# Decoder layer on one core: all engines' work lists reordered, PSUM banks reassigned, max and score groups of opposite rows placed side by side

## What is computed

```python
def attn(x):                      # 16 heads of 16
    q = (layernorm(x, qn) @ Wq + bq) * scale ; k, v = layernorm(x, kvn) @ Wkv + bkv
    q, k = rotary(q, norm(x)), rotary(k, norm(x))      # rotated, then layernorm per head
    w = softmax(where(causal, layernorm(q) @ layernorm(k).T / 4, min))
    return (w @ v) @ Wo + bo
def xattn(x, enc):                # the 64 positions are features, the 256 features positions
    q, k, v = split(x.T @ w_in.T + b_in)               # 8 heads of 8, 256 x 256 scores
    o = softmax(where(band, q @ k.T / sqrt(8), min)) @ v
    return (relu((o @ w_out.T + b_out).T) * enc) @ w_ct + b_ct
def ffn(x):                       # weights quantised to three levels in groups of 64
    gate, up = split(x @ ternary(w_gate_up).T)
    return rms_norm(silu(gate) * up) @ ternary(w_proj).T
x = layernorm(x + attn(x)); x = layernorm(x + xattn(x, ctx)); x = layernorm(x + ffn(x))
```

## Time and profile before

| | before |
|---|---|
| median of three runs | 899.84 us (898.8 to 900.99) |
| the profiled execution | 899.05 us |
| its span on the core | 897.3 us |
| busy PE / POOL / DVE / ACT | 819.0 / 760.4 / 762.2 / 653.7 us |
| mean granted clock of TensorE | 0.974 |

### The profile page before, as it was taken

How to read it: one execution, slowest core, us unless ns; L and a number is a source line. 1 busy time by engine, 2 the same in 40 slices (tenths; PEclk the granted TensorE clock), 3 DMA queues, 4 the chain that set the end, 5 groups by cost and what they waited for, 6 DMA issues and landing times.

```text
span 897.3 us, 23809 instructions
## 1 busy us (share of the span) xinstructions
PE 819.0 (91%) x9618; PEld 493.9 (55%) x9618; DVE 762.2 (85%) x1495; ACT 653.7 (73%) x1171; POOL 760.4 (85%) x879
## 2 busy tenths in 40 slices
PE   3779998899999999999999999999999999889885
PEld 1334555455566655665666665666666665545442
DVE  4699988888989999998998999999999998767663
ACT  1356567667878888888887887888888888756763
POOL 5498889978999999999999999999999987544741
PEclk9889999999999999999999999999999999988998
DMA  7000111111233333322222222233333332223333
GB/s 249 12 7 14 45 46 30 39 32 35 66 67 73 73 73 73 72 67 67 69 65 59 66 65 66 68 66 72 73 73 73 67 68 67 61 60 67 54 85 86
DMA packets 125029, 57.64 MB, mean 64 GB/s; under 512 B 93044, under 2 KB 124020, under 8 KB 124920
## 3 DMA queue, kind: packets, MB, share of 16 engines
q1 hardware_dynamic: 124920, 56.12, 27.5%
HBM read 13.62 MB, written 4.19 MB: 20 GB/s over the span
## 4 chain that ended last, share of the span: by engine, by line
PE 48%; DVE 15%; POOL 15%; SPq 11%; DMA 6%; ACT 3%; issue 2%; POOLq 0%; DVEq 0%
PE ps L741 6%; SPq L299 5%; PE ps L710 4%; POOL hsum L2142 4%; PE ps L669 3%; PE ps L561 3%; DMA xin<-in_x 3%; PE ps L794 3%; PE ps L825 3%; PE ps L618 3%; PE ps L549 3%; PE ps L810 2%; DVE rowmax L2644 2%; PE ps L600 2%; POOL prob L2180 2%
## 5 line engine op out<-in xcount | busy, mean ns | idle before, releaser
L1550 ACT ACTIVATE prob<-ps 128x768 f32<-128x768 f32 x256 | 207.5, 811 | 73.7 <-PE ps L710 72.0
L2644 DVE TENSOR_REDUCE rowmax<-ps 128x4 f32<-128x768 f32 x256 | 241.8, 945 | 17.0 <-PE ps L669 15.6
L2142 POOL TENSOR_TENSOR hsum<-hsum,minus_half 128x32 f32<-128x32 f32 x32 | 176.8, 5526 | 1.1 <-DVE hsum L2569 1.0
L2178 POOL TENSOR_SCALAR_AFFINE_SELECT prob<-prob 128x512 f32<-128x512 f32 (+1 forms) x128 | 111.7, 873 | 31.8 <-ACT prob L1550 31.5
L2180 POOL TENSOR_SCALAR_AFFINE_SELECT prob<-prob 128x1024 f32<-128x1024 f32 (+1 forms) x128 | 112.0, 875 | 0.0
L741 PE MATMUL ps<-prob,v_pad 128*32 128x192 f32 x2048 | 97.8, 332 | 0.5 <-POOL prob L2180 0.3
L710 PE MATMUL ps<-q_rows,k_rows 32*128 32x192 f16 x1024 | 86.5, 247 | 12.7 <-ACT prob L1550 6.6
L669 PE MATMUL ps<-k_rows,q_rows 31*128 31x192 f16 x1024 | 86.5, 246 | 6.8 <-DMA k_rows<-qk_lo 4.4
L741 PEld LDWEIGHTS ps<-prob,v_pad 128*32 128x32 f32 x2048 | 60.5, 111 | 25.0 <-issue 9.7
L710 PEld LDWEIGHTS ps<-q_rows,k_rows 32*128 32x128 f16 x1024 | 30.9, 93 | 77.4 <-issue 27.7
L810 PE MATMUL ps<-wgu,xsplitT 128*128 128x512 bf16 x256 | 67.6, 387 | 5.6 <-DVE hid L2713 2.6
(11 more groups left out here) (154 smaller groups left out, 2031.1 us busy)
## 6 DMA issues: line engine op xcount, KB each, us to landing
v_swap<-v_own SPq DMA_DIRECT2D x64, 68.0 KB, 2.1
xin<-in_x SPq DMA_DIRECT2D x32, 128.0 KB, 2.3
q_rows<-qk_hi SPq DMA_DIRECT2D x64, 64.0 KB, 2.0
k_rows<-qk_hi SPq DMA_DIRECT2D x64, 64.0 KB, 2.0
enc<-in_ctx SPq DMA_DIRECT2D x32, 128.0 KB, 2.3
out<-yout SPq DMA_DIRECT2D x32, 128.0 KB, 1.9
prob<-in_w_guT SPq DMA_DIRECT2D x4, 512.0 KB, 7.1
q_rows<-qk_lo SPq DMA_DIRECT2D x32, 64.0 KB, 2.0
```

The lines of the kernel that those rows point to most:

```text
L1550: copy(prob[:, 2 * c:2 * c + 2, :, :].rearrange("p u a b -> p u (a b)"), ps[:, STB:STB + 2, 0:2 * QW], ACT.Exp, scale=float(XD) ** -0.5).t ...
L2142: g.tensor_tensor(hsum[:, t.two, 1, :], hsum[:, t.two, 0, :], minus_half[:, :], ALU.pow).then_inc(S["head_pow3"], 1)
L2178: g.affine_select(out=lead, in_=lead, compare_op=ALU.is_ge, fill=0.0, base=BAND - 64 * kb, pattern=[[0, 8], [1, cut]], channel_multiplier=-1)
L2644: v.tensor_reduce(of_head[:, hq:hq + 2, 2 * row_of(ng):2 * row_of(ng) + 2], ps[:, MXB:MXB + 2, 0:2 * QW].rearrange("p j (a b) -> p j a b", ...
```

## The change

The lists of all five engines are written in another order, in prologue, step and epilogue; the lags between tiles and the PSUM banks are set anew, and with the banks the waits for a bank's last reader. No operation of the computation is added or taken away (fillers: 153 instead of 150). Relative to qk the tiles of most steps stay the same; the border of the step moves by two.

PE's step after: ct(-9), mx4(-6), st5(-7), xproj(-5), mx5, st6, gate0(-10), val0(-7), wo(-4), pt1(-3), mx6, st7, hf(-8), up0(-10), down(-12), mx7, xnT(0), gate1(-10), maxT(-6), mx0(-5), qkT(-2), up1(-10), qk(0), mx1(-5), st0(-6), s(-2), pt0(-3), st1, mx2, val1(-7), st2, z(-8), tr(-7), st3, o(-3), st4, mx3, v(-1), aT(-3). Six times a group of even number and one of odd number stand side by side (mx4 and st5, mx5 and st6, mx6 and st7, mx1 and st0, st1 and mx2, st4 and mx3); before it is once (st0 and mx1).

On DVE x_stats moves behind max2, on POOL x2_lo behind the rotation of the same step, on ACT the order around xproj becomes exp5, qk_hi, v_pad, h_hi. Core of the diff:

```diff
-XNT_B, QK_B, V_B, QKT_B, PT0_B, PT1_B, AT_B, WO_B, MAXT_B, TR_B = 6, 7, 5, 6, 7, 5, 7, 5, 7, 5
-HF_B, Z_B, CT_B, GATE0_B, GATE1_B, UP0_B, UP1_B, DOWN_B, S_B, O_B = 6, 7, 6, 7, 7, 5, 5, 6, 5, 6
+XNT_B, QK_B, V_B, QKT_B, PT0_B, PT1_B, AT_B, WO_B, MAXT_B, TR_B = 5, 7, 5, 6, 7, 6, 6, 5, 5, 5
+HF_B, Z_B, CT_B, GATE0_B, GATE1_B, UP0_B, UP1_B, DOWN_B, S_B, O_B = 7, 6, 7, 7, 7, 5, 5, 7, 5, 6
...
             def put_hT(t, c):
+                if c == 0:
+                    sp.wait_ge(S["h_hi"], t.at(1, 1))
                 if c == 1:
                     sp.wait_ge(S["h_lo1"], t.at(1, 1))
                 do_hT(t, c)
...
             def step(at):
-                t = at(-3)
-                if t:
-                    put_vswap(t)
                 t = at(0)
                 if t:
                     put_xload(t)
                 t = at(-7)
                 if t:
                     put_maxrow(t)
-                t = at(-12)
+                t = at(-10)
+                if t:
+                    put_xT(t)
+                t = at(-11)
                 if t:
                     put_hT(t, 0)
-                t = at(-10)
-                if t:
-                    put_xT(t)
+                t = at(-5)
+                if t:
+                    put_rep_hi(t)
+                    put_rep_lo(t)
                 t = at(-14)
                 if t:
                     put_out(t)
-                t = at(-5)
-                if t:
-                    put_rep_lo(t)
-                    put_rep_hi(t)
-                t = at(-8)
+                t = at(-6)
                 if t:
                     put_enc(t)
                 t = at(-11)
                 if t:
                     put_hT(t, 1)
+                t = at(-2)
+                if t:
+                    put_vswap(t)
 
...
             def put_xnT_ps(t):
                 pe.wait_ge(S["xn"], t.at(1, 1))
-                if t.has(12):
-                    pe.wait_ge(S["y3"], t.back(12).at(1, 1))
+                if t.has(10):
+                    pe.wait_ge(S["hid0"], t.back(10).at(1, 1))
                 do_xnT_ps(t)
             def put_qk_ps(t):
-                if t.has(6):
-                    pe.wait_ge(S["max_hi"], t.back(6).at(1, 1))
+                if t.has(10):
+                    pe.wait_ge(S["silu1"], t.back(10).at(1, 1))
                 do_qk_ps(t)
 
             def put_v_ps(t):
+                if t.has(6):
+                    pe.wait_ge(S["heads"], t.back(6).at(1, 1))
                 do_v_ps(t)
 
             def put_qkT_ps(t):
-                if t.has(-2):
-                    pe.wait_ge(S["xnT"], t.back(-2).at(1, 1))
                 pe.wait_ge(S["qkn"], t.at(1, 1))
+                if t.has(1):
+                    pe.wait_ge(S["pt1"], t.back(1).at(1, 1))
                 do_qkT_ps(t)
             def put_pt_ps(t, c):
                 if c == 1:
-                    if t.has(1):
-                        pe.wait_ge(S["y1"], t.back(1).at(1, 1))
+                    pe.wait_ge(S["s_exp"], t.at(1, 1))
                 if c == 0:
-                    if t.has(5):
-                        pe.wait_ge(S["zr"], t.back(5).at(1, 1))
+                    if t.has(-3):
+                        pe.wait_ge(S["qk"], t.back(-3).at(1, 1))
                 do_pt_ps(t, c)
 
...
             def put_maxT_ps(t):
-                if t.has(4):
-                    pe.wait_ge(S["silu1"], t.back(4).at(1, 1))
+                if t.has(-6):
+                    pe.wait_ge(S["xnT"], t.back(-6).at(1, 1))
+                pe.wait_ge(S["max"], t.at(8, 8))
                 do_maxT_ps(t)
             def put_hf_ps(t):
-                if t.has(-3):
-                    pe.wait_ge(S["qk_lo"], t.back(-3).at(1, 1))
+                if t.has(2):
+                    pe.wait_ge(S["silu0"], t.back(2).at(1, 1))
                 do_hf_ps(t)
             def put_z_ps(t):
-                if t.has(-8):
-                    pe.wait_ge(S["qk"], t.back(-8).at(1, 1))
+                if t.has(-6):
+                    pe.wait_ge(S["s_sub"], t.back(-6).at(1, 1))
                 do_z_ps(t)
             def put_gate_ps(t, c):
                 if c == 0:
-                    if t.has(-6):
-                        pe.wait_ge(S["aT"], t.back(-6).at(1, 1))
                     pe.wait_ge(s_xT, t.at(16, 16))
                 if c == 1:
-                    pe.wait_ge(S["silu0"], t.at(1, 1))
+                    if t.has(2):
+                        pe.wait_ge(S["y3"], t.back(2).at(1, 1))
                 do_gate_ps(t, c)
...
             def put_up_ps(t, c):
                 if c == 0:
-                    if t.has(-7):
-                        pe.wait_ge(S["pt1"], t.back(-7).at(1, 1))
                     if t.has(-6):
                         pe.wait_ge(S["y1"], t.back(-6).at(1, 1))
                 if c == 1:
-                    pe.wait_ge(S["hid0"], t.at(1, 1))
+                    if t.has(-4):
+                        pe.wait_ge(S["max_hi"], t.back(-4).at(1, 1))
                 do_up_ps(t, c)
 
...
             sum_gains()
             turn_bias()
             carry_bias()
-            keep_warm(9)
             sum_weights(0)
             pe.wait_ge(S["xn"], tile[0].at(1, 1))
             do_xnT_ps(tile[0])
-            keep_warm(2)
             pe.wait_ge(S["xnT"], tile[0].at(1, 1))
-            do_v_ps(tile[0])
             do_qk_ps(tile[0])
...
-            clear_rows()
             pool.wait_ge(S["x_stats"], tile[0].at(1, 1))
             do_x_pow(tile[0])
             pool.wait_ge(S["x_stats"], tile[1].at(1, 1))
             do_x_pow(tile[1])
+            clear_rows()
+            pool.wait_ge(S["qk"], tile[0].at(1, 1))
+            do_rotated(tile[0])
             do_xbo(tile[0])
             do_xbo(tile[1])
-            pool.wait_ge(S["qk"], tile[0].at(1, 1))
...
+            scale_weights()
             spread_gains()
-            scale_weights()
-            fold_bias()
-            scale_gains()
             dve.wait_ge(s_x[tile[0].buf], tile[0].dma(1))
             do_x_stats(tile[0])
+            fold_bias()
             hold_bias()
             dve.wait_ge(s_x[tile[1].buf], tile[1].dma(1))
             dve.wait_ge(S["x_stats"], tile[0].at(1, 1))
             do_x_stats(tile[1])
-            add_bias()
             dve.wait_ge(S["x_pow"], tile[0].at(1, 1))
             do_xn_nb(tile[0])
             dve.wait_ge(S["x_pow"], tile[1].at(1, 1))
             do_xn_nb(tile[1])
+            scale_gains()
             quantise(0, 1)
             quantise(0, 2)
             dve.wait_ge(S["qk_ps"], tile[0].at(1, 1))
             do_qk(tile[0])
             quantise(0, 3)
+            add_bias()
             quantise(0, 4)
             quantise(1, 1)
+            dve.wait_ge(S["qk_ps"], tile[1].at(1, 1))
+            do_qk(tile[1])
             dve.wait_ge(S["rotated"], tile[0].at(1, 1))
             do_centred(tile[0])
```

2050 lines of the change are left out of this document (1047 added, 1003 removed).

## The result

The changed kernel is slower: 927.66 us (median of 4, 924.23 to 937.11) against 899.32 us for the kernel before, ratio 1.0331 with a 95% interval of 1.0247 to 1.0414. The forecast was 893.5 us with a range up to 907: the sign was wrong, and the time lies 21 us outside the range. What happened is rival C, SP's queue, in the place where the prediction had put it, and a loss in the end that no rival had.

A forecast was written before the change was run, and what follows sets the result against it. The prediction took POOL to bound the steady loop, at 23.60 us a tile. From the profiled 899.05 us, −5 (start), +2 (SP's queue) and −2.5 (drain) gave 893.5; own range 887 to 898, wide range 878 to 907.

The forecast's parts named there:

- rival C: SP's queue, with hT0 and its wait on h_hi ahead of maxrow, becomes the bound: about 905 us; chance 0.26.
- What bounds the kernel: Steady loop, 250 to 716 us: POOL is the bound, as it waits only 3.2 us in 466.
- the floor: POOL's period without waits, 23.60 us a tile in the steady stretch; savings on PE alone cannot go below it.
- the loop through SP: Steady step's chain xproj, SP, maxrow, st0, xproj: closes in 23.7 to 24.2 us, 23.9 taken.
- Part 1, the pairs: PE: six opposite-row pairs run together, saving 1.0 us a step, worth at most 0.22 us a steady tile.
- Part 2, SP's queue: Steady stretch: maxrow issued 11.9 us behind xproj instead of 10.1; +0.1 us on 21 tiles, +2 us.
- Part 3, the start: Prologue: clears moved, filler dropped, tile 0's rotation 6 us earlier; −5 us kept.
- The bound of −4: Start, smaller end of the gain: moved clears hold one of DVE's quantising operations for 2 us.
- Part 4, the banks: New bank waits in PE's list: taken as nothing, covered by 1.6 us a step.
- Part 5, the drain: Behind the last rotation: five steps at most 1.0 us shorter each, half taken, −2.5 us.
- The prediction's own test: Signs of rival C: POOL's period over 24.2 us, POOL waiting for qk, st0's waits behind maxrow from 15 to over 30.
- D: No change: pairs only move PE's waits to DVE's evacuations, head start used up: 898 to 901 us; chance 0.12.

The follow-up runs named there:

- b_no_pow: The kernel before with POOL's power of the head norms replaced by one multiplication: 906.04 us, ratio 1.0065.
- a_hT0_out_back: The changed kernel with SP's transpose hT0 back behind maxrow and out ahead of the row copies: 903.96 us, ratio 1.0034 to the kernel before.
- a_back_flip: a_hT0_out_back with score groups exchanged, which undoes the six opposite pairs: 925.17 us, ratio 1.0263 to the kernel before.
- b_flip: The kernel before with opposite pairs alone, by exchange of score groups, no list reordered: 902.46 us, ratio 1.0018.

## Why the prediction was wrong, point by point

**What bounds the kernel (open for the kernel before; the floor was too high).** "POOL is the bound there" was read from 3.2 us of waits in 466. That one of two full engines (PE 458.64, POOL 451.50 of 466) hardly waits shows that its list fits the period, not that it sets it, and b_no_pow, meant to decide it, changed DVE's work too. The floor, "nothing that only PE saves can push a steady tile below 23.60", has the wrong number: with hT0 back POOL does the same work in 23.44 us a tile and waits 0.5 us in 466. So POOL may well be the bound where nothing else is longer. In the changed kernel something was: the loop through SP.

**Part 1, the pairs (the saving right for the list after, its worth wrong).** PE saves about what was forecast where all six pairs run together: busy 22.7 us a step in a_hT0_out_back against 23.9 in a_back_flip. In the changed kernel itself it is five pairs: mx1 and st0 run together in none of 20 tiles, as mx1 goes ahead and st0 waits for maxrow's row. PE's st0 there:

```profile
519.49 0.34 PE L715 MATMUL ps<-q_rows,k_rows 32*128 32x192 f16 x4 [1.24 <-DMA q_rows<-negmax]
```

"In the steady stretch it is worth nothing beyond 0.22 us a tile" agrees with b_flip, which saves PE only 0.3 us a step. In the new lists the pairs carry 0.62 us a step and 21 us in all (a_back_flip). The price of a step that PE saves had to be asked of the list after, not of the profile before.

**Part 2, SP's queue (mechanism right, size wrong; this is the step that made the steady stretch slower).** 11.9 us to maxrow's issue were forecast, 11.69 measured. 13.9 to 14.4 us to st0 were forecast; measured 12.9 to 15.0 by tile, a mean of 14.0. So the queue's part was right. The rest of the loop, from st0 to the end of xproj, was costed at 9.85 and is 10.5 in the mean. The two make 24.5, and 23.9 was taken. The term that was mis-sized is PE's part: it was summed from PE's durations alone, while the new list puts z behind DVE's s_sub and v behind heads, and its weight loads wait for DVE to empty the maxima's banks (the rows of waits above). Which of these waits makes the 0.65 us was not tried; with hT0 back it is still 10.4 to 10.6. At 24.5 rival C priced the steady stretch at +14; by qk_hi, just behind xproj, the changed kernel was 6.3 us ahead at tile 8 and 10.6 behind at tile 31, 16.9 in all.

**Part 3, the start (right, but what is left of it behind the fill was luck).** −6 was forecast for the first rotation, −6.4 came. PE's first sum was forecast at 8.4 us and starts at 8.72. The bound of −4 was the clears that hold DVE, and they do. Timeline of DVE beside the moved clears (17.83 to 23.09 us):

```profile
17.99 5.14 DVE L2530 TENSOR_SCALAR kgain<-lncol 128x2 f32<-128x2 f32 x4
19.52 3.61 DVE L2554 TENSOR_SCALAR hT<-ps 128x1024 bf16<-128x1024 f32 x1
```

The four of scale_gains (kgain), 0.62 us together in the kernel before, last until both clears are over, and quantise's first operation ends 1 ns behind the last of them: 3.61 us instead of 1.22. It was 2.4 us on the path, as the bound had it; that −6.4 came nonetheless means that the fillers and what they covered were worth about 6.2 (6.4 and 2.4, less the 2.6 of PE's first sum), not the −3 taken. That POOL's interface is shared with VectorE is what the Trainium skill says ("GPSIMD Engine Reference", section "1. Specifications"), and these rows agree; but what was held is not "the one with two inputs" that the prediction took, for scale_gains multiplies one tensor, and whether it ran in one of the modes that the page names no run shows. "I keep −5" came out as −6.1 at tile 12 of this execution; in five of the ten executions with this start and these lists 0.6 us or less was left there.

**Part 4, the banks (wrong).** "I take nothing for them" left out v behind heads and z behind s_sub; the first stands in the chain of the changed kernel above, and the weight loads of the two waited 6.9 and 7.5 us in 466. What each bank wait costs alone was not tried.

**Part 5, the drain (wrong, and the largest term).** −2.5 forecast, +21.6 measured. Seven of it is the loop again, up to the last xproj (10.6 late there, 3.6 at the last rotation). The other 14.6 lie behind. The step that failed is the one that took the drain as five steps, each shorter by what PE saves there. The prediction did not look at where the border of the step cuts the last tile's groups, which the diff showed: mx(-7) became mx(-5) and mx(-6). In its place the runs show the last maximum of tile 31 coming 12 us later behind its xproj, and some 2 us of granted clock; that the cut is the cause stays open.

**The rivals.** C's mechanism came, with 0.26. Its price of 905 had the gains of start and drain in it, +13 − 7.5; without the drain's gain, and with the end's loss of 14.6, it comes to about 922, near the 924.23 of the profiled execution. The prediction's own test held in part: POOL's period went over 24.2 (24.33), POOL waits for qk, and maxrow's issue stands 11.69 behind xproj (it said 11.9 in every case); but st0's waits for that row, weight loads and products together, went from 16.4 us to 23.7 and not "over 30". D's sign came as well, weight loads waiting for DVE's maxima (4.6 to 28.4 us), but they wait as long in a_hT0_out_back (28.8), which steps in 23.39; they are not what made the changed kernel slow.
